# A decoder's combine stage: the addition of x2 moved from VectorE to GpSimd, with VectorE one group behind

## What is computed

```python
x = _layernorm(x + attn(x))                 # softmax features, linear attention
x = _layernorm(x + cross_attn(x, ctx))      # this result is x2
# mixture of experts: 8 experts, the top 2 of each token, and 8 shared ones
routed = einsum('te,etd->td', gates, out_e)
x = _layernorm(x2 + 0.5 * shared + 0.5 * routed)
```

## Time and profile before

| what | value |
|---|---|
| median of three runs | 850.24 us (846.84 to 852.47) |
| profiled execution, its own time | 843.65 us |
| its span, first to last instruction | 841.9 us |
| mean granted PE clock | 0.927 |
| busy: PE, DVE, ACT, POOL | 713.6, 487.4, 481.5, 461.6 us |

### The profile page before, as it was taken

The page is one execution under the profiler, slowest core; times in us unless marked ns, Lnnn a source line. Parts: engine busy times, 40 slices in busy tenths (PEclk is TensorE's granted clock), DMA queues, the critical chain, the costliest instruction groups (busy, mean ns, idle before and its releaser), DMA issues.

```text
span 841.9 us, 16996 instructions
## 1 busy us (share of the span) xinstructions
PE 713.6 (85%) x5112; PEld 650.7 (77%) x5113; DVE 487.4 (58%) x1435; ACT 481.5 (57%) x1441; POOL 461.6 (55%) x471
## 2 busy tenths in 40 slices
PE   5789999874999996898888888989889888999950
PEld 3668888763788885898888888888889887898750
DVE  3798999864899753433434343334333434446896
ACT  5889999821399722544445344445444444544796
POOL 3378988852111155266766666666666666541322
PEclk9999999875999997899999999999999999999985
DMA  5457555523211232011111111111111112215573
GB/s 172 151 176 227 176 181 168 151 75 102 74 51 51 76 84 64 24 41 42 44 44 41 44 41 44 44 44 41 41 44 44 44 42 42 38 58 154 149 217 109
DMA packets 87238, 72.57 MB, mean 86 GB/s; under 512 B 10067, under 2 KB 72411, under 8 KB 87195
## 3 DMA queue, kind: packets, MB, share of 16 engines
q1 hardware_dynamic: 77808, 53.43, 21.5%
q0 software_dynamic: 9088, 18.63, 8.3%
q10 hardware_dynamic: 298, 0.01, 0.0%
HBM read 50.14 MB, written 21.89 MB: 86 GB/s over the span
## 4 chain that ended last, share of the span: by engine, by line
PE 46%; issue 7%; DVE 5%; ACT 2%; another core or an unknown queue 1%; DMA 1%; ACTq 0%; POOLq 0%; POOL 0%; SPq 0%; DVEq 0%
PE bank L1325 15%; PE bank L1293 9%; PE bank L1294 9%; PE bank L1295 9%; PE bank L1285 2%; DVE xg L1609 2%; DVE f_st L1626 1%; DVE z L1620 1%; DVE f_hT L1597 1%; ACT xg L1571 1%; DMA f_x2T<-x2T_cols 1%; PE bank L1513 0%; PE bank L1512 0%; PE bank L1511 0%
## 5 line engine op out<-in xcount | busy, mean ns | idle before, releaser
L1403 DVE TENSOR_TENSOR e_hT<-e_sg,bank 128x512 f32<-128x512 f32 x142 | 97.7, 688 | 258.5 <-PE bank L1295 109.4
L1266 POOL DMA_INDIRECT y_rows<-e_y,dst_tab x142 | 148.0, 1042 | 108.5 <-ACT e_y L1357 75.8
L1293 PE MATMUL bank<-e_x_hi,e_w_hi 128*128 128x256 f32 x568 | 179.0, 315 | 29.9 <-issue 27.0
L1294 PE MATMUL bank<-e_x_lo,e_w_hi 128*128 128x256 f32 x568 | 167.1, 294 | 8.6 <-issue 7.8
L1295 PE MATMUL bank<-e_x_hi,e_w_lo 128*128 128x256 f32 x568 | 166.9, 294 | 4.2 <-issue 4.0
L1258 POOL DMA_INDIRECT xg<-x_rows,src_tab x130 | 130.1, 1001 | 55.1 <-issue 36.0
L1351 ACT ACTIVATE e_sg<-bank 128x512 f32<-128x512 f32 x142 | 84.6, 596 | 116.7 <-PE bank L1295 76.0
L1325 PE MATMUL bank<-w,e_hT 128*128 x1136 | 142.7, 279 | 4.7 <-issue 4.4
L1293 PEld LDWEIGHTS bank<-e_x_hi,e_w_hi 128*128 128x128 f32 x568 | 114.0, 201 | 37.1 <-issue 32.7
L1325 PEld LDWEIGHTS bank<-w,e_hT 128*128 128x128 f32 x1136 | 136.5, 196 | 6.0 <-issue 5.7
L1295 PEld LDWEIGHTS bank<-e_x_hi,e_w_lo 128*128 128x128 f32 x568 | 114.3, 201 | 9.5 <-issue 9.2
(11 more groups left out here) (172 smaller groups left out, 1544.2 us busy)
## 6 DMA issues: line engine op xcount, KB each, us to landing
yk<-y_rows SPq DMA_DIRECT2D x16, 512.0 KB, 4.4
xT_in<-in_xT_dram SPq DMA_DIRECT2D x16, 256.0 KB, 3.3
x_res<-in_x_dram SPq DMA_DIRECT2D x16, 256.0 KB, 3.6
w_in<-in_L_ffn_w_e_dram SPq DMA_DIRECT2D x16, 256.0 KB, 3.0
c_in<-in_ctx_dram SPq DMA_DIRECT2D x16, 256.0 KB, 2.9
cT_in<-in_ctxT_dram SPq DMA_DIRECT2D x16, 256.0 KB, 3.2
x_rows<-x SPq DMA_DIRECT2D x16, 256.0 KB, 2.4
x2T_cols<-x2T SPq DMA_DIRECT2D x16, 256.0 KB, 2.7
```

What stands on the lines that cost most here:

```text
L1266: nc.gpsimd.indirect_dma_start(y_rows, bass.IndirectOffsetOnAxis(dst_tab[:, n:n + 1], 0), y[b % R][:, t, :], None).then_inc(scattered[b % ...
L1293: nc.tensor.matmul(at, w_hi[r % 2][:, w], x_hi[r][:, :], start=True, stop=False)
L1294: nc.tensor.matmul(at, w_hi[r % 2][:, w], x_lo[r][:, :], start=False, stop=False)
L1403: nc.vector.tensor_tensor(hT[par][:, half * HC:(half + 1) * HC, :].rearrange("p c n -> p (c n)"), sg[half][:, :], bank[2 + half][:, :], AL ...
```

## The change

`total` on DVE becomes the four gated multiply-adds, from `part` to `z`. `part` is now made by POOL (`with_x2`): first plus x2. The second yk row is read by `total`, so SP's load waits for `z_ok`. DVE's total(g-1) stands in iteration g, `spreads` after the second shared step. POOL does with_x2(g) ahead of root(g-1).

```diff
         def load(g):
             if g >= R:
-                sp.wait_ge(part_ok, g - R + 1)
+                sp.wait_ge(z_ok, g - R + 1)
...
-        def second(g):
-            dve.wait_ge(first_ok, g + 1)
-            for t in range(GT):
-                last = nc.vector.scalar_tensor_tensor(part[g % 2][:, t, :], yk[g % R][:, t, 1, :],
-                                                      gates[:, 1, g * GT + t:g * GT + t + 1],
-                                                      first[g % 2][:, t, :], ALU.mult, ALU.add)
-            last.then_inc(part_ok, 1)
-
         def total(g):
             if g >= 4:
                 dve.wait_ge(res_ok, g - 3)
-            if g >= EARLY:
-                dve.wait_ge(added, g - EARLY + 1)
             dve.wait_ge(part_ok, g + 1)
-            nc.vector.tensor_tensor(z[g % R][:, :, :], part[g % 2][:, :, :],
-                                    x2_all[:, g * GT:(g + 1) * GT, :], ALU.add).then_inc(z_ok, 1)
+            for t in range(GT):
+                last = nc.vector.scalar_tensor_tensor(z[g % R][:, t, :], yk[g % R][:, t, 1, :],
+                                                      gates[:, 1, g * GT + t:g * GT + t + 1],
+                                                      part[g % 2][:, t, :], ALU.mult, ALU.add)
+            last.then_inc(z_ok, 1)
...
         for g in range(NG + 2):
             shared(LEAD + 2 * g)
-            if g < NG:
-                second(g)
+            if 1 <= g <= NG:
+                total(g - 1)
+            shared(LEAD + 2 * g + 1)
             if 1 <= g <= NG:
                 spreads(g - 1)
             if g >= 2:
                 shifts(g - 2)
-            shared(LEAD + 2 * g + 1)
-            if g < NG:
-                total(g)
             if 1 <= g <= NG:
                 moments(g - 1)
                 variances(g - 1)
...
+        def with_x2(g):
+            pool.wait_ge(first_ok, g + 1)
+            if g >= EARLY:
+                pool.wait_ge(added, g - EARLY + 1)
+            if g >= 2:
+                pool.wait_ge(z_ok, g - 1)
+            nc.gpsimd.tensor_tensor(part[g % 2][:, :, :], first[g % 2][:, :, :], x2_all[:, g * GT:(g + 1) * GT, :],
+                                    ALU.add).then_inc(part_ok, 1)
+
...
+            if g < NG:
+                with_x2(g)
             if g >= 1:
                 root(g - 1)
```

## The result

The median after is 861.09 us (859.26 to 862.04, six runs), before it was 850.31 us (846.84 to 852.47, six runs). The ratio is 1.0127 with a 95% interval of 1.0103 to 1.0151: slower, by 10.8 us. The forecast was 857.6, 7.4 us slower, in a range of 848 to 863.

A forecast was written before the change was run, and what follows sets the result against it. DVE was taken to set the pace after 811 us and share the lead with ACT before. 8.05 us for late casts less 0.65 from there to the end gave +7.4: 850.24 to 857.6 us, range 848 to 863.

The forecast's parts named there:

- R: SyncE's queue: yk is released an iteration later, delaying the x2T loads behind its loads; second cast 8.05 us late.
- P: POOL's add collides with DVE instructions on two SBUF operands, holding them 1.06 us each time.
- The casts: ACT's two x_high casts, waiting for late x2T loads: at 787.8 in place of 783.19, and 802.6 in place of 794.55.
- The collision in iterations with hidden: DVE's total: POOL's add gets in before the fourth multiply-add, 0.87 us lost against 0.60 saved each time.
- The bound from above for this term: Collision of POOL's add with DVE: the whole 1.40 us of the longest x_low row, 0.3 us more each time.
- The tail: DVE iterations 9 to 15, without hidden: shift held, groups 2.85 us, 3.0 with add_shared; 20.3 us in place of 22.07.
- The end: After iteration 15, where total(15) now comes: 9.6 us to the span's end in place of 8.8.
- The sum: Whole kernel: +8.05 - 0.65 = +7.4 us, profiled span 841.9 to 849.3, median 850.24 to 857.6.
- rival D: All of the forecast and slow x2T loads: each cast another 2 to 3 us late, 862 us; chance 0.16.
- A: The shared port costs nothing for these forms: +0.2 us, 850.4; chance 0.12.
- B: The x2T loads don't matter, the port does; slack makes up the later cast: +1.5 us, 851.7; chance 0.12.
- C: Neither cost hurts and the removed DVE work counts; tail falls to ACT's 2.70 us: about -5 us, 845; chance 0.05.

The follow-up runs named there:

- R alone: Kernel before with SyncE's load(g) waiting for second(g-3) in place of second(g-4), one iteration later: ratio 1.0098, combine 83.3 us.
- the held POOL: Kernel after with POOL's with_x2(g) held until DVE has finished total(g-1): ratio 1.0043, combine 80.1 us.
- the early loads: Kernel after with the two late x2T loads issued two SyncE iterations earlier: ratio 0.9981, combine 75.0 us.
- with two of them: Kernel after with the two late x2T loads issued earlier and with_x2(g) held until total(g-1) is done: ratio 0.9955, combine 72.8 us.
- with three: Kernel after with early x2T loads, with_x2 held behind total, and DVE's shifts(g-2) moved behind variances(g-1): ratio 0.9939, 844.71 us, combine 71.1 us.
- the memset: Kernel after with POOL's add replaced by a memset of part that reads nothing, leaving first and x2 out: ratio 1.0010, combine 77.8 us.

## Why the prediction was right, and where it was off

**Direction and both mechanisms: right.** R alone, put into the kernel before, costs 7.0 us, and R and P taken out of the kernel after give 12.2 us. The forecast named both with these places. The second cast waited 7.00 us, though, where 5 to 6 was said.

**The casts.** The forecast had the first 4.6 us late and the second 8.05. On after's scale (9.17 us later) that is 796.97 and 811.77; they came at 797.26 and 812.23, 0.29 and 0.46 later.

**The collision in iterations with hidden: undersized.** "POOL gets in before the fourth multiply-add": in iterations 1, 3, 5 and 7 it got in before the third. In iteration 7 with_x2 began 1.24 us after the issue of the variance (820.74 - 819.50), just as the third was due, and total began 0.04 us later than I had summed; so the third was held for POOL's read and the fourth came on top. From the start of the four to the next instruction are 2.14 us (820.22 to 822.36), a loss of 1.10 where I took 0.87. In iterations 4, 6 and 8 it did get in before the fourth, and that cost 1.04 (815.52 to 817.60 is 2.08): begun while the third ran, POOL's add took 1.40 to 1.45 us, and the sum had 1.27. Iterations 6 to 8 lasted 14.69 us (814.91 to 829.60) and not 14.15. The bound from above for this term, 0.3 us more each time, held.

**The tail.** Its groups are 2.89 and 3.06 us long (829.60 to 832.66 has add_shared), forecast 2.85 and 3.0; iterations 9 to 15 took 20.56 us (829.60 to 850.16) and not 20.3. The shift was held, as said. The end took 9.64 us, forecast 9.6. These terms, 0.44 us at hidden(18), 0.54, 0.26 and 0.04, are the 1.3 us between the forecast of 7.4 and the 8.7 of the combine.

**The sum.** The other 2.1 us of the measured 10.8 lie in front of the combine, and the forecast had no term for them. It carried the difference of one profile over to a median; on the third chip that holds within about 1 us. The measured 861.09 is just over the forecast's own spread (853 to 861) and nearer to the 862 of rival D than to 857.6: by the number D did better, and only the traces tell that its slow loads didn't happen.

**The rivals.** A (the port costs nothing) fell with the held POOL: 4.9 us. B (the x2T loads don't matter) fell with the early loads: 10.0 us. C, the gain, is real but needs edits: with two of them the combine is 3.5 us under before, with three 5.2, and the tail at 2.68 us, where it was said to fall to 2.70, comes only when no two-operand instruction of DVE meets POOL's add. D's slow landings didn't happen: from issue to cast were 4.41 and 4.33 us (812.23 - 807.90).

**The Trainium skill.** SBUF — State Buffer, Who interferes with whom, would hold DVE for the whole POOL instruction, 0.2 us more each time. With the collision at 820.74 POOL ends at 822.02; the third multiply-add ends at 822.17 (1.43 us from 820.74), and a free one takes 0.35, so it started at about 821.82, by that estimate: 0.2 us before POOL's record ends. Whether the rest belongs to the record or to the port no run here shows. Nor is every POOL record that reads SBUF such a hold: beside the root (829.77 to 830.83) the four multiply-adds of 829.60 take 1.14 us. The same section has a GpSimd instruction that only writes leave a two-input DVE one alone, and the memset shows it.

## What to carry to other kernels

When the last reader of a buffer moves to a later place, look at what is queued behind the load that waits for it: here the yk loads had three iterations to spare, and the two small loads in the same queue had none. Work moved from DVE to POOL was free here only where it fell beside DVE instructions with one SBUF operand. A single wait that puts POOL's add behind the multiply-adds was worth 4.9 us; look too at what the add meets in its new place, since here it held the shift for longer, and only a third edit took that out. Compare profiles stage by stage, by the start of the stage: two spans 17.9 us apart held a change of 8.7.

## What the runs showed of the hardware

A POOL add that reads SBUF (1.28 us) holds a DVE multiply-add with two SBUF operands for about 1.08 us (1.43 for a free 0.35, at 820.74), and the small shift too (0.53 in place of 0.14); a POOL memset of the same tile (0.53 us) holds none. It works the other way too: begun during a multiply-add, POOL's add took 1.40 to 1.45 us in place of 1.26 to 1.29. `hidden`, with one operand in PSUM, is never held: 0.67 to 0.69 us. The root, POOL's power on 128x4, took 1.12 to 1.17 us in the tail of the version with all three edits, where it begins within 0.1 us of the multiply-adds, and 1.01 to 1.07 in the kernels before and after (1.06 in after's tail, beside them too); why it is longer there wasn't tested:

```profile
833.98 1.17 POOL L1675 TENSOR_TENSOR f_rs<-f_ve,minus_half 128x4 f32<-128x4 f32 x1 [0.17 <-DVE f_ve L1630]
```

What I hadn't expected at all is how far apart chips are: the same kernel before has medians of 850.4, 843.04 and 777.35 us on three of them, while its combine is 76.3, 76.4 and 76.35 us. Nearly all of it lies in the expert loop: from the loop's first weight cast (L1341) to the first gate are 443.7 us on the first chip and 381.8 on the third, a difference of 61.9 of the 65.3 us between the two starts of the combine. The granted clock alone, 0.95 and 1.00 over the loop, doesn't give that much.
